# Regrouping the small steps around the first batch in the first stage of a two-layer kernel on one core

## The chip, the cores and the metric

The kernel runs on one core of a Trainium2 chip. The metric is the device time of one execution in microseconds (us). The core has five engines that run side by side, each with its own queue in program order: PE (TensorE, matrix products and transposes), DVE (VectorE), ACT (ScalarE), POOL (GpSimd) and SP, which here only issues DMAs. They wait for each other through semaphores.

## The reference

Two layers work on x of 4 batches x 1024 tokens x 128 columns. Each has an attention half and a feed-forward half, with modulation from a small product of c:

```python
mod = (silu(c) @ wmod)                       # six rows: sa, ca, ga, sb, cb, gb
h = layernorm(x) * (1 + ca) + sa
x = x + ga * attention(h)
h = layernorm(x) * (1 + cb) + sb
x = x + gb * ffn(h)
```

What the change touches is layer 0. Its attention is linear: Q = h W_Q^T, K = h W_K^T, M = K^T h, J = Q M / sqrt(128) + h, then a layernorm of J with gamma and beta. Its feed-forward is a choice of 2 of 8 experts for each token: gates = h gate_w^T + gate_b, the two largest, a softmax over the two, and for each chosen expert gelu(h w1 + b1) w2 + b2, weighted. Layer 1 (softmax attention over anchors, a gated ternary feed-forward) follows.

## The kernel before

**Stages.** From 0 to about 150 us the kernel does the first attention, the second norm and the routing of all four batches, and splits the expert weights into two parts. Then 23 tiles of rows, sorted by expert, go through the experts (to about 290 us). The rest is layer 1. All data of a batch is a tile of 128 partitions x 8 x 128 columns (`xa[:, b]`); a batch is handled in 8 column tiles, and most steps are in two halves g = 0, 1 of four tiles.

**Batch b of layer 0**, in the order of its dependences (engine in brackets):
- `first_stats(b)` [DVE]: 8 bn_stats of x, 8 bn_aggr, one addition of epsilon (`ve_L0a`). `rstd("L0a", b)` [POOL, L593]: the power -0.5. `minus_mean` [DVE, L1108]: `nmr_L0a`. `z_made(b)` [ACT, L737]: normalized rows z, 8 instructions; of batch 0 the first half is done by DVE (`half_normalized`, L1090).
- `z_transposed` [PE, L1653], `h0T_out` [ACT], `h0_back` [PE], `h0_out` [ACT], `gram` [PE, L1686], `gram_out` [ACT], `product` [PE, L1691], which gives P in PSUM. `first_half(b)` is ACT's part of this.
- `centred(b)` [DVE, L1116 to L1123]: `pm` and `pcat` from P. `jn_raw(b)` and `jn_centred(b)` [PE, L1703]. `beta(b)` [DVE, L1099] adds a row to `xa[:, b]`; for batch 1 POOL does it (L630) after the rows have come back from HBM.
- `inner_stats(b)` [DVE] on jn in PSUM, a root (`rstd("L0i", b)` on POOL for batches 0 and 1, Newton steps on DVE for 2 and 3), `residual_1(b)` [DVE, L1143], `second_stats(b)` [DVE], a root (POOL for batch 0, DVE for the others), `minus_mean` (`nmr_L0b`), `zb_made(b)` [ACT], `zb_transposed` [PE], `h1T_out` [ACT], `gates(b)` [PE, L1735].
- `choose(b)` [DVE, L1155 to L1170]: 14 small instructions to the chosen experts (`sel`). `ranks(b)` [PE]. `positions(b)` [DVE, L1186 to L1192]: `pos`. `scatter(b, ts)` [POOL, L601]: 16 indirect DMAs that write the rows of h1 to `rows_by_expert` in HBM.

**Expert weights.** They come in four quarters: SP loads `raw[q % 2]`, ACT rounds it (`expert_hi(q)`, 128 x 2048), DVE subtracts (`remainders(q, i)`, L1279, two operations of 128 x 1024), SP stores the parts to `w_split`. SP loads quarter q + 2 only behind the store of quarter q.

**Order.** Every queue's order is written out by hand. On DVE the steps of batch 0 are interleaved with statistics of later batches, the tables for routing, and `remainders(0, 0)` and `(0, 1)`; from batch 1 on there is a loop. On POOL the roots of all batches stand ahead of scatter(0), and nothing but the 64 scatters follows until layer 0's expert stage. SP issues all loads one after another: silu's input, `wm` in two halves, `xa[0]`, eight small ones (`gateb` is the last, and PE's `ww` product, L1769, waits for all of them), `xa[1..3]`, then `raw`.

## Time and profile before

| | us |
|---|---|
| median of 3 runs | 786.03 (785.18 to 786.83) |
| the profiled execution | 785.84 |
| its span, first to last instruction | 784.1 |

| engine | busy us | share of the span | instructions |
|---|---|---|---|
| PE | 656.5 | 84% | 2985 |
| DVE | 570.3 | 73% | 1443 |
| ACT | 400.9 | 51% | 698 |
| POOL | 271.5 | 35% | 227 |

The page's second part cuts the span into 40 slices of 19.6 us. In the first seven PE is busy 5, 5, 7, 7, 8, 4 and 1 tenths, and its granted clock falls from 9 to 5 and 6 tenths in the slices from 78 to 137 us; from about 150 us on PE is the busiest engine nearly throughout. So a share of 84% says little of the first stage, and it has to be read from timelines and from the chain of waits. Times count from the span's start.

### The profile page before, as it was taken

Reading aid. Unit: us, or ns where it says so; the run is one execution under the profiler, and the core shown is the slowest. Engines: PE = TensorE matmul, PEld = TensorE weight load, DVE = VectorE, ACT = ScalarE, POOL = GpSimd, SP = SyncE. Lnnn points to the kernel's source line nnn. Section 1 sums busy time; section 2 is a strip of 40 time slices with the busy share of each in tenths; the row PEclk is TensorE's granted clock in tenths of the full one; section 3 lists DMA queues with packets and bytes.
Section 4 is the critical chain, followed back from the end, with each engine's and each line's share of the span. In section 5 each row is a group of like instructions: output and inputs, shape, how many; then the busy total and the mean of one; then the engine's idle time right before and its main releaser. Section 6 shows DMA issues by size and latency. Waiting matters only on the chain.

```text
span 784.1 us, 9644 instructions
## 1 busy us (share of the span) xinstructions
PE 656.5 (84%) x2985; PEld 474.0 (60%) x2985; DVE 570.3 (73%) x1443; ACT 400.9 (51%) x698; POOL 271.5 (35%) x227
## 2 busy tenths in 40 slices
PE   5577841199999995679989899999899899899897
PEld 3467731178888874345468656468555478556575
DVE  4988767568877746976977686976786866793763
ACT  3455443167777742325276444375444485452573
POOL 6346767400000016687202276202475220341100
PEclk9896655589999995889999999999999999999999
DMA  5631277778899721000000000000100000000000
GB/s 210 206 101 45 108 277 288 252 254 266 268 280 337 229 80 31 23 21 20 8 1 0 34 21 28 1 0 1 37 24 22 0 1 1 27 1 1 0 1 28
DMA packets 25780, 69.26 MB, mean 88 GB/s; under 512 B 5297, under 2 KB 8385, under 8 KB 24385
## 3 DMA queue, kind: packets, MB, share of 16 engines
q1 hardware_dynamic: 21632, 60.24, 22.3%
q0 software_dynamic: 4096, 8.40, 3.4%
q8 instruction: 25, 0.41, 0.2%
q14 instruction: 27, 0.21, 0.1%
HBM read 46.46 MB, written 22.16 MB: 88 GB/s over the span
## 4 chain that ended last, share of the span: by engine, by line
PE 61%; DVE 21%; issue 5%; ACT 4%; POOL 4%; DMA 3%; SPq 1%; DVEq 0%; ACTq 0%; POOLq 0%
PE ps L1657 15%; PE ps L1653 9%; PE ps L1659 8%; PE ps L1661 6%; PE ps L1660 6%; PE ps L1913 6%; DVE stats L1051 3%; POOL rows_by_expert L601 2%; PE ps L1901 2%; PE ps L1931 2%; DVE lsum L1506 2%; PE ps L1703 2%; DVE ring L1538 2%; DMA raw<-in_w 1%; DVE yb L1438 1%
## 5 line engine op out<-in xcount | busy, mean ns | idle before, releaser
L642 POOL DMA_INDIRECT yb<-y_by_expert,ypos x64 | 63.8, 997 | 158.3 <-DMA y_by_expert<-ysb 142.6
L1657 PE MATMUL ps<-hid,fh 128*128 128x512 f32 x256 | 103.3, 404 | 5.1 <-DVE hid L1522 5.1
L1659 PE MATMUL ps<-hid,fh 128*128 128x512 f32 x256 | 101.4, 396 | 0.0
L690 POOL TENSOR_TENSOR misc<-misc,ring 128x1024 f32<-128x1024 f32 x28 | 66.0, 2356 | 35.5 <-DVE ring L1512 30.4
L601 POOL DMA_INDIRECT rows_by_expert<-h,pos x64 | 68.9, 1076 | 25.3 <-issue 18.5
L1522 DVE TENSOR_TENSOR hid<-ring,hid 128x512 fp32r<-128x512 f32 x56 | 38.6, 689 | 41.3 <-ACT hid L930 39.7
L1657 PEld LDWEIGHTS ps<-hid,fh 128*128 128x128 f32 x256 | 48.1, 188 | 20.9 <-DVE hid L1522 10.4
L1913 PE MATMUL ps<-ring,hn 128*128 128x512 f32 x112 | 55.4, 617 | 5.0 <-DVE ring L1512 5.0
L1931 PE MATMUL ps<-attnT,cmat 128*128 128x512 f32 x128 | 56.9, 593 | 0.0
L987 ACT ACTIVATE ring<-ps 128x1024 f32<-128x1024 f32 x32 | 32.8, 1024 | 44.2 <-PE ps L1901 44.0
L1659 PEld LDWEIGHTS ps<-hid,fh 128*128 128x128 f32 x256 | 48.2, 188 | 10.5
L1491 DVE TENSOR_REDUCE nmax<-ps 128x16 f32<-128x1024 f32 x32 | 39.1, 1221 | 18.1 <-PE ps L1661 18.1
L716 ACT ACTIVATE attnT<-ps 128x512 f32<-128x512 f32 x64 | 36.9, 597 | 21.0 <-PE ps L1653 20.2
L1403 DVE TENSOR_TENSOR hid<-ring,hid 128x512 fp32r<-128x512 f32 (+1 forms) x46 | 28.1, 610 | 26.5 <-ACT hid L725 26.5
L1060 DVE TENSOR_TENSOR hid<-ring,hid 128x512 fp32r<-128x512 f32 (+1 forms) x70 | 44.7, 639 | 2.4
L1506 DVE TENSOR_REDUCE lsum<-ring 128x16 f32<-128x1024 f32 x32 | 38.9, 1214 | 5.7 <-ACT ring L987 5.4
L929 ACT ACTIVATE ring<-ps,fs 128x512 f32<-128x512 f32 x32 | 22.0, 686 | 40.4 <-PE ps L1659 40.0
L1653 PE MATMUL ps<-ident,ring 128*128 128x128 f32 x224 | 33.1, 278 | 7.5 <-DVE hTa L1477 7.3
L1931 PEld LDWEIGHTS ps<-attnT,cmat 128*128 128x128 f32 x128 | 23.7, 191 | 25.0 <-issue 23.9
L1512 DVE TENSOR_TENSOR ring<-ring,lrec 128x1024 f32<-128x1024 f32 x28 | 37.8, 1350 | 1.0
L1657 PE MATMUL ps<-hT,wbuf 128*128 128x512 f32 (+1 forms) x92 | 34.8, 378 | 3.3 <-issue 1.6
L1653 PEld LDWEIGHTS ps<-ident,ring 128*128 128x128 f32 x224 | 25.5, 142 | 18.9 <-issue 18.8
(323 smaller groups left out, 1681.2 us busy)
## 6 DMA issues: line engine op xcount, KB each, us to landing
wbuf<-w_split SPq DMA_DIRECT2D x46, 512.0 KB, 5.4
w_split<-parts SPq DMA_DIRECT2D x4, 2048.0 KB, 7.0
raw<-in_w SPq DMA_DIRECT2D x8, 512.0 KB, 8.9
xs<-rows_by_expert SPq DMA_DIRECT2D x16, 256.0 KB, 5.6
y_by_expert<-ysb SPq DMA_DIRECT2D x16, 256.0 KB, 4.8
ffn_raw<-in_ffn SPq DMA_DIRECT2D x1, 2816.0 KB, 11.2
rows_by_expert<-zeros SPq DMA_DIRECT2D x9, 256.0 KB, 2.3
xa<-in_x SPq DMA_DIRECT2D x4, 512.0 KB, 6.3
```

The costliest lines, as they stand in the source:

```text
L601: gp.indirect_dma_start(disp, bass.IndirectOffsetOnAxis(pos[:, b, k, t:t + 1].bitcast(U32), 0), h1[:, b % 2, t, :], None).then_inc(scatter ...
L642: gp.indirect_dma_start(yb[:, k, t, :], None, ydisp, bass.IndirectOffsetOnAxis(ypos[:, b, k, t:t + 1].bitcast(U32), 0))\
L690: gp.tensor_tensor(asum, asum, ring[:, 2 * (t % 2):2 * (t % 2) + 2, :] .rearrange("p a n -> p (a n)"), ALU.add).then_inc(*pool_asum.raise_(t))
L1060: v.tensor_tensor(dst_lo, src, f(dst_hi), ALU.subtract).then_inc(*ev.raise_(job))
L1506: settle(b, v.tensor_reduce(lsum[:, :], exponentials(t), X, ALU.add))
L1653: last_ = te.transpose(ps[0:rows_, bank, i * 128:(i + 1) * 128], s, ident[:, :])
L1657: te.matmul(out_, w(0), x(0), start=first, stop=False)
L1659: return te.matmul(out_, w(0), x(1), start=False, stop=last_)
L1660: te.matmul(out_, w(0), x(1), start=False, stop=False)
L1661: return te.matmul(out_, w(1), x(0), start=False, stop=last_)
L1913: last_ = te.matmul(ps[:, 6 + h, :], hn[:, t, :], attention(t, h), start=t == 0, stop=t == T - 1)
L1931: last_ = te.matmul(ps[:, 2 + g, :], cmat[:, k, :], attnT[:, k, g * GW:(g + 1) * GW], start=k == 0, stop=k == AC - 1)
```

## The change

It reorders layer 0's work around batch 0 and 1:

- SP: `xa[0]` is loaded ahead of the first `wm`, `xa[1]` ahead of the second `wm` and the small loads.
- DVE: `first_stats` is cut in two, `first_stats` (bn_stats) and `first_sums` (bn_aggr and epsilon), with a second buffer `next_stats`. The bn_stats of batch 1 stand ahead of batch 0's `norm_ready`, those of batch 2 behind `first_sums(1)`; `first_sums(2)` stands between `inner_stats(0)` and `residual_1(0)`; `first_stats(3)` and `first_sums(3)` move ahead of `choose(0)`. `residual_1(0)`, `second_stats(0)` and `centred(1)` move ahead of the `modt` columns. Tables that routing needs later (`thr`, `unit`, `upto`) move behind batch 1's `norm_ready`, `onehot` behind `y_positions`. `residual_1(1)` is in two halves around `positions(0)`.
- POOL: it takes over both remainders of quarter 0 (behind `zb` of batch 0), and the roots of `L0a` for batch 2 and of `L0b` for batch 0 change places around the addition to `xa[1]`.
- ACT: `z_made(2)` stands behind `first_half(1)`, `z_made(3)` behind `h1_out` of batch 0, each one batch sooner.
- PE: `jn_raw(1)` goes ahead of `zb_transposed(0)`, `jn_centred(1)` is in two halves, `gates` waits for each half of h1T by itself, and `z_transposed(2, 0)` goes behind `ranks(0)`.

```diff
@@ SP
             load(silu[:, :], ins["cT"], l_mod)
+            load(xa[:, 0], by_tile(ins["x"][0]), l_x[0])
             load(wm[:, 0, :], ins["wmod"][:, 0:768], l_mod)
-            load(xa[:, 0], by_tile(ins["x"][0]), l_x[0])
+            load(xa[:, 1], by_tile(ins["x"][1]), l_x[1])
             load(wm[:, 1, :], ins["wmod"][:, 768:1536], l_mod1)
...
             for q in range(4):
-                sp.wait_ge(*w_lo.done((q, 1)))
+                sp.wait_ge(*(w_lo if q else pool_lo).done((q, 1)))
@@ POOL
             rstd("L0i", 0)
-            rstd("L0b", 0)
+            rstd("L0a", 2)
             pool.wait_ge(l_rows, 16)
             pool.wait_ge(*act_z.done((1, 1)))
             gp.tensor_tensor(xa[:, 1], xa[:, 1], over_tiles(R_GBETA, 1, T), ALU.add).then_inc(pool_beta, 1)
-            rstd("L0a", 2)
+            rstd("L0b", 0)
+
+            pool.wait_ge(*zb_done(0, 0))
+            pool.wait_ge(*w_hi.done(0))
+            for i in range(2):
+                gp.tensor_tensor(parts[0][:, :, i, 1, :], raw[0][:, i], f(parts[0][:, :, i, 0, :]), ALU.subtract)\
+                    .then_inc(*pool_lo.raise_((0, i)))
             rstd("L0i", 1)
             rstd("L0a", 3)
@@ ACT
             first_half(1)
+            z_made(2)
...
-                if b + 2 < B:
-                    z_made(b + 2)
+                if b == 0:
+                    z_made(3)
                 tanh(b)
@@ DVE
+            def first_sums(b, of=stats):
+                if b:
+                    dve.wait_ge(*dve_nmr["L0a"].done(b - 1))
+                if b == 1:
+                    dve.wait_ge(*z_done(0, 0))
+                aggregated("rows", "L0a", 0, T, of).then_inc(*dve_var["L0a"].raise_(b))
...
             first_stats(0)
+            first_sums(0)
...
+            first_stats(1)
             norm_ready("L0a", 0)
             half_normalized("L0a", z, "z")
...
-            first_stats(1)
+            first_sums(1)
+            first_stats(2, next_stats)
...
             inner_stats(0)
-            remainders(0, 0)
+            first_sums(2, next_stats)
+            residual_1(0)
+            minus_mean("L0a", 2)
+            second_stats(0)
+            centred(1)
...
-            residual_1(0)
-            second_stats(0)
+            norm_ready("L0b", 0)
+            half_normalized("L0b", zb, "zb")
...
-            remainders(0, 1)
-            norm_ready("L0b", 0)
-            half_normalized("L0b", zb, "zb")
-            centred(1)
-            v.tensor_copy(onehot[:, :], oh_f[:, :])
-            first_stats(2)
-            inner_stats(1)
...
-            norm_ready("L0a", 2)
             choose(0)
-            first_stats(3)
+            minus_mean("L0a", 3)
+            residual_1(1, (0,))
             positions(0)
-            residual_1(1)
-            norm_ready("L0a", 3)
+            residual_1(1, (1,))
             second_stats(1)
             norm_ready("L0b", 1)
...
             y_positions()
+            v.tensor_copy(onehot[:, :], oh_f[:, :])
@@ PE
             product(1)
+            jn_raw(1)
             for g in gs2:
                 zb_transposed(0, g)
-            jn_raw(1)
+            jn_centred(1, (0,))
             pe.wait_ge(*dve_setup.done("jv"))
             gates(0)
-            jn_centred(1)
```

(`inner_stats(1)`, `first_stats(3)` and `first_sums(3)` follow the tables `order`, `erow` and `tot`, ahead of `choose(0)`.)

## Rows read from the trace of the kernel before

**Rows 1.** Chain that ended last, in order of time: start us, us, what.
```profile
95.08 10.43 DMA raw<-in_w
...
146.73 2.82 DMA rows_by_expert<-h,pos
```
**Rows 2.** Timeline of POOL: start us, us, engine line op out<-in xcount [idle before <-releaser].
```profile
53.75 1.24 POOL L601 DMA_INDIRECT rows_by_expert<-h,pos  x1 [0.21 <-issue]
...
76.82 0.96 POOL L601 DMA_INDIRECT rows_by_expert<-h,pos  x1 [1.99 <-DVE pos L1192]
...
101.51 0.96 POOL L601 DMA_INDIRECT rows_by_expert<-h,pos  x1 [3.87 <-DVE pos L1192]
...
123.80 0.95 POOL L601 DMA_INDIRECT rows_by_expert<-h,pos  x1 [0.92 <-DVE pos L1192]
```
**Rows 3.** Timelines of DVE and ACT, first loads; columns as above.
```profile
7.69 1.64 DVE L1051 BATCH_NORM_STATS2 stats<-xa 128x6 f32<-128x128 f32 x8 [7.69 <-DMA xa<-in_x]
...
12.00 0.37 DVE L1108 SCALAR_TENSOR_TENSOR nmr_L0a<-mv_L0a,rs_L0a 128x8 f32<-128x8 f32 x1 [1.64 <-POOL rs_L0a L593]
...
6.33 0.21 ACT L798 ACTIVATE silu<-silu 128x8 f32<-128x8 f32 x1 [4.26 <-DMA wm<-in_wmod]
```
**Rows 4.** Timeline of PE.
```profile
13.62 0.49 PE L1769 MATMUL ps<-wkq 128*128 128x128 f32 x2 [1.23 <-DMA gateb<-in_gate_b]
```
**Rows 5.** Timelines of POOL and DVE, 10 to 38 us.
```profile
10.31 1.66 POOL L593 TENSOR_TENSOR rs_L0a<-ve_L0a,neghalf 128x8 f32<-128x8 f32 x1 [4.45 <-DVE ve_L0a L1056]
...
25.46 2.55 POOL L593 TENSOR_TENSOR rs_L0i<-ve_L0i,neghalf 128x8 f32<-128x8 f32 x1 [5.98 <-DVE ve_L0i L1056]
...
34.52 2.71 POOL L630 TENSOR_TENSOR xa<-xa,rows 128x1024 f32<-128x1024 f32 x1
...
25.29 1.22 DVE L1279 TENSOR_TENSOR parts<-raw,parts 128x1024 fp32r<-128x1024 f32 x1
...
28.11 2.16 DVE L1143 SCALAR_TENSOR_TENSOR xa<-ps,rs_L0i,xa 128x128 f32<-128x128 f32 x8 [1.05 <-issue]
...
32.67 0.17 DVE L1056 TENSOR_SCALAR ve_L0b<-mv_L0b 128x8 f32<-128x8 f32 x1
...
34.95 2.30 DVE L1108 SCALAR_TENSOR_TENSOR nmr_L0b<-mv_L0b,rs_L0b 128x8 f32<-128x8 f32 x1
```
**Rows 6.** The instructions of line 1495: durations ns min/median/max, first and last start.
```profile
L1495 DVE CAST m<-nmax x32: 174/304/2991, 311.3 to 700.8; 128x16 fp32r<-128x16 f32 x32
```
**Rows 7.** Timeline of DVE, 45 to 60 us.
```profile
45.88 0.22 DVE L1155 TENSOR_TENSOR gt<-ps,gateb 128x64 f32<-128x64 f32 x1
...
49.29 1.65 DVE L1051 BATCH_NORM_STATS2 stats<-xa 128x6 f32<-128x128 f32 x8
...
52.63 0.17 DVE L1192 CAST pos<-posf 128x16 int32<-128x16 f32 x1
...
59.72 0.17 DVE L1108 SCALAR_TENSOR_TENSOR nmr_L0b<-mv_L0b,rs_L0b 128x8 f32<-128x8 f32 x1
```
**Rows 8.** Timeline of PE; then windows: busy of each engine, granted clock, DMA, GB/s.
```profile
60.66 3.79 PE L1703 MATMUL ps<-pm,h0T 128*128 128x128 f32 x16 [4.12 <-DVE pm L1116]
...
84.89 2.05 PE L1703 MATMUL ps<-pm,h0T 128*128 128x128 f32 x16 [0.38 <-DVE pm L1116]
...
50.00:60.00 10.00, 5.95 (x43) 4.81 (x43) 9.33 (x59) 6.27 (x12) 6.67 (x6) 0.98 0.09 29
60.00:66.00 6.00, 5.34 (x24) 5.09 (x24) 3.91 (x17) 3.77 (x9) 4.77 (x5) 0.50 0.13 44
```
**Rows 9.** Timelines of DVE and ACT, 64 to 85 us.
```profile
64.58 1.68 DVE L1051 BATCH_NORM_STATS2 stats<-ps 128x6 f32<-128x128 f32 x8 [1.95 <-PE ps L1703]
...
84.54 0.29 DVE L1116 SCALAR_TENSOR_TENSOR pm<-ps,ident 128x128 f32<-128x128 f32 x1 [3.00 <-PE ps L1691]
...
73.91 3.17 ACT L737 ACTIVATE z<-xa,nmr_L0a,rs_L0a 128x128 f32<-128x128 f32 x8
```
**Rows 10.** Timeline of DVE, start of the expert stage.
```profile
153.29 0.42 DVE L1393 TENSOR_TENSOR hT<-ps,hT 128x256 fp32r<-128x256 f32 x1 [7.10 <-ACT hT L725]
```

More of the change, by code:

```diff
@@ L297, in build @@
         pool_beta = sem("pool_beta")
-        w_hi, w_lo = Once(sem("w_hi"), range(4)), Once(sem("w_lo"), [(q, i) for q in range(4) for i in range(2)])
+        w_hi, w_lo = Once(sem("w_hi"), range(4)), Once(sem("w_lo"), [(q, i) for q in range(1, 4) for i in range(2)])
+        pool_lo = Once(sem("pool_lo"), [(0, i) for i in range(2)])
         f_hi, f_lo = Once(sem("f_hi"), range(4)), sem("f_lo")
@@ L469, in _ @@
                 load(dst, src, l_small)
-            for b in range(1, B):
+            for b in range(2, B):
                 load(xa[:, b], by_tile(ins["x"][b]), l_x[b])
@@ L1099, in beta, with first_stats @@
                 settle("rows", v.tensor_tensor(xa[:, b], xa[:, b], row, ALU.add))
-            def first_stats(b):
+            def first_stats(b, to=stats):
                 dve.wait_ge(l_x[b], 16)
-                norm_stats("rows", "L0a", 0, [xa[:, b, t, :] for t in ts]).then_inc(*dve_var["L0a"].raise_(b))
+                tile_stats("rows", [xa[:, b, t, :] for t in ts], to)
+            def first_sums(b, of=stats):
[4 more added lines that the diff above has]
+                aggregated("rows", "L0a", 0, T, of).then_inc(*dve_var["L0a"].raise_(b))
             def minus_mean(k, b):
@@ L1133, in inner_stats, with residual_1 @@
                 norm_stats("rows", "L0i", 0, [jn(t, 2) for t in ts]).then_inc(*dve_var["L0i"].raise_(b))
-            def residual_1(b):
-                if b == 1:
+            def residual_1(b, halves=gs2):
+                if b == 1 and 0 in halves:
                     dve.wait_ge(pool_beta, 1)
-                if b < POOL_ROOTS["L0i"]:
+                if b < POOL_ROOTS["L0i"] and 0 in halves:
                     dve.wait_ge(*pool_rs["L0i"].done(b))
-                for g in gs2:
+                for g in halves:
                     dve.wait_ge(*pe_jn.done((b, g)))
@@ L1145, in residual_1 @@
                     last.then_inc(*dve_x1.raise_((b, g)))
-                dve.wait_ge(*dve_x1.done((b, 1)))
+                if 1 in halves:
+                    dve.wait_ge(*dve_x1.done((b, 1)))
             def second_stats(b):
@@ L1328, in _ @@
             settle("setup", v.tensor_copy(jv[:, :], ps[:, 6, 128:160]))
-            residual_1(0)
-            second_stats(0)
+            norm_ready("L0b", 0)
+            half_normalized("L0b", zb, "zb")
             v.tensor_scalar(order[:, :], jv[:, 0:E], -1.0, float(E), ALU.mult, ALU.add)
             v.tensor_scalar(erow[:, :], jv[:, 0:E], float(REGION), None, ALU.mult)
-            v.tensor_scalar(thr[:, :], jv[:, 0:E], float(GW), None, ALU.mult)
-            v.tensor_scalar(tot[:, :], jv[:, 0:E], 0.0, None, ALU.mult)
-            settle("setup", v.tensor_scalar(unit[:, :], jv[:, 0:NT], 0.5, WIDE / 2.0, ALU.mult, ALU.add))
-            v.tensor_tensor(unit[:, :], unit[:, :], jv[:, 0:NT], ALU.min)
-            v.tensor_tensor(upto[:, :, :], jv[:, 0:2 * E].unsqueeze(1).broadcast_to([128, 2 * E, 2 * E]),
-                            jv[:, 0:2 * E].unsqueeze(2).broadcast_to([128, 2 * E, 2 * E]), ALU.is_le)\
-                .then_inc(*dve_setup.raise_("jv"))
-            dve.wait_ge(*dve_setup.done("jv"))
-            remainders(0, 1)
-            norm_ready("L0b", 0)
-            half_normalized("L0b", zb, "zb")
-            centred(1)
-            v.tensor_copy(onehot[:, :], oh_f[:, :])
-            first_stats(2)
-            inner_stats(1)
+            v.tensor_scalar(tot[:, :], jv[:, 0:E], 0.0, None, ALU.mult).then_inc(*dve_setup.raise_("jv"))
+            inner_stats(1)
+            first_stats(3)
+            first_sums(3)
+            dve.wait_ge(*dve_setup.done("jv"))
             def both(q):
@@ L1351, in both @@
                     remainders(q, i)
-            norm_ready("L0a", 2)
             choose(0)
-            first_stats(3)
+            minus_mean("L0a", 3)
+            residual_1(1, (0,))
             positions(0)
-            residual_1(1)
-            norm_ready("L0a", 3)
+            residual_1(1, (1,))
             second_stats(1)
             norm_ready("L0b", 1)
+            v.tensor_scalar(thr[:, :], jv[:, 0:E], float(GW), None, ALU.mult)
+            settle("setup", v.tensor_scalar(unit[:, :], jv[:, 0:NT], 0.5, WIDE / 2.0, ALU.mult, ALU.add))
+            v.tensor_tensor(unit[:, :], unit[:, :], jv[:, 0:NT], ALU.min)
+            settle("setup", v.tensor_tensor(upto[:, :, :], jv[:, 0:2 * E].unsqueeze(1).broadcast_to([128, 2 * E, 2 * E]),
+                                            jv[:, 0:2 * E].unsqueeze(2).broadcast_to([128, 2 * E, 2 * E]), ALU.is_le))
             for b in range(1, B):
@@ L1712, in jn_raw, with jn_centred @@
                     rows_times(b, 2, pm[:, b % 2, :], g, pe_raw)
-            def jn_centred(b):
+            def jn_centred(b, halves=gs2):
                 pe.wait_ge(*dve_pcat.done(b))
-                for g in gs2:
+                for g in halves:
                     if b:
```

19 lines of the change are left out of this document (12 added, 7 removed).

## The prediction

> **What bounds the kernel now.** The span is 784.1 us, and behind 152 us PE is the chain; the change touches only what lies ahead of the first expert tile. So the views to read are those of 0 to 160 us. First the chain in order of time: DVE steps, then the `raw` load of the fourth quarter of expert weights, then POOL's scatters; the last lands 2.82 us after 146.73, and only then can the first expert tile come [rows 1]. So two streams set the end: the dependent steps over DVE, ACT and PE that give `pos` of each batch, and POOL's 64 scatters, which need `pos`. Second, POOL's timeline: batches of scatters start at 53.75, 76.82, 101.51 and 123.80, with 1.99, 3.87 and 0.92 us idle before the last three [rows 2]. About 0.3 us of each is the ordinary spacing, so POOL has 5.9 us to give; what goes beyond must come from an earlier scatter(0). Third, DVE's timeline, where each idle time names what is late.
>
> **The loads.** `xa[0]` now comes ahead of the first `wm`, and `xa[1]` ahead of the second and of all small loads. DVE idles 1.64 us before batch 0's `nmr_L0a` [rows 3]; the bn_stats of batch 1 now fall there, those of batch 2 take their old place, and DVE's work up to `pm` of batch 0 stays the same. But PE's `ww` product waits for the last small load, `gateb`, at 13.62 [rows 4], and all of batch 0 is behind it. One more issue and 512 KB now go ahead of `gateb`. Bounds: +0.4 us if only the issue counts, and +1.4 us if the bytes count (`xa[0]`, as large, landed 1.36 us behind `wm` [rows 3]). I take **+0.6**: `gateb` came alone, long after its neighbours' bytes, so it is nearer to the first.
>
> **Batch 0 up to nmr_L0b.** Before, `remainders(0,0)` (1.22 us at 25.29) ran while POOL wanted `rs_L0i`: POOL took 2.55 us where its root before took some 1.65 (10.31 to 11.97), and DVE idled 1.05 before `residual_1(0)` at 28.11 [rows 5]. The remainder is gone, and `first_sums(2)` fits beside the root: **-0.95**. New on POOL, ahead of `rstd("L0b",0)`, is `rstd("L0a",2)`, about 1.65, and with it the `xa[1]` addition comes sooner: 2.71 us at 34.52 before [rows 5], of which some 2.2 are its own (DVE's remainder held it back until 35.0). It will run from about 29.4 to 31.6, and DVE wants `minus_mean("L0a",2)` at 29.9. The trace shows what such a meeting costs: `nmr_L0b`, on 8 columns, took 2.30 us from 34.95, just until POOL's addition ended [rows 5]. So **+1.9** (bounds 0, if DVE is first, and 2.2). `ve` of `second_stats(0)` then ends at 34.3 instead of 32.84. Before, 4.4 us passed from there to the end of `nmr_L0b` at 37.25, with the second remainder and POOL's addition in the way [rows 5]. Now it waits for the root alone, 1.65, beside which `centred(1)` and the `modt` columns fit: 1.9, **-2.55**. Sum 0.6 - 0.95 + 1.9 - 2.55 = -1.0: `nmr_L0b(0)` at 36.2.
>
> A rule of the Trainium skill speaks against this regrouping: "SBUF — State Buffer", section "Who interferes with whom", calls the ports that VectorE shares with GpSimd an exclusive lock, which copies, casts and tensor_scalar within SBUF need as well as operations with two SBUF inputs. The trace agrees for two inputs (2.30 us) and for a cast, median 304 ns and at most 2991 [rows 6]; for the `ve` tensor_scalar no row shows it.
>
> **From zb to choose(0).** `remainders(0,*)` go to POOL behind `zb`: two operations of 2.2 to 2.7 us by the addition's row, 37.4 to about 42. Queued behind them on POOL are the roots `L0i`(1) and `L0a`(3) and scatter(0); `L0a`(3) would end near 46.5, before DVE asks. SP's queue waits for them with the store of quarter 0 and the `raw` loads of quarter 2 behind it, some 7 us later than now; ACT wants these only at 75. PE does `jn_raw(1)` ahead of `zb`'s transposes, which therefore come some 0.3 to 1 us behind `zb`. DVE has `order`, `erow`, `tot`, `inner_stats(1)`, `first_stats(3)` and `first_sums(3)`, 5.2 us, and waits some 0.9 for `jn_raw(1)` by these times. One of these DVE steps may be caught by POOL: bounds 0 and 2.2 us, I take 1.1, halfway, since nothing shows which of the two comes first. `choose(0)` starts at 44.3 instead of 45.88 [rows 7]. With no catch it would be 43.5, where PE's `gates(0)` are due too.
>
> **choose(0) to nmr_L0b(1).** `first_stats(3)`, 2.44 us from 49.29 on with its bn_aggr, is out of this stretch; `thr`, `unit`, `upto` (0.75) move behind it; `positions(0)` waits 0.3 for PE's ranks and lies between the halves of `residual_1(1)`. So `pos(0)` comes at 50.2 instead of 52.8 [rows 7], scatter(0) starts at 51.0 instead of 53.75 [rows 2], and `nmr_L0b(1)` ends at 56.3 instead of 59.9 [rows 7]: **-3.6**. With the tables, `centred(2)` comes at 57.5, and `jn_raw(2)` on PE at 57.9 instead of 60.66 [rows 8]: -2.8.
>
> **ACT.** `z_made(3)` takes the slot of `z_made(2)` ahead of `first_half(2)`, 3.2 us each, so P of batch 2 comes near 56.5, as before: just not late. `expert_hi(1)` ends at 57.9, then comes `zb_made(1)`, 2 us sooner than now; `gates(1)` then end near 64, and DVE needs them at 64.6.
>
> **jn_raw(2).** It took 3.79 us at 60.66, with a granted clock of 0.50 from 60 to 66 us, the lower level, 1.2 GHz; the same work took 2.05 at 84.89, and 50 to 60 us had 0.98 [rows 8]. PE had stood idle 4.1 us ahead of it. Now the gap is 1.4 us, and I expect the higher level: `inner_stats(2)` at 60.0 instead of 64.58 [rows 9], **-4.6**; at the lower one, -2.8.
>
> **Batch 3's first half.** DVE waited 3.00 us for P(3) until 84.54, because ACT made `z(3)` only from 73.91 on (3.17 us) and another 7.4 us went by to P [rows 9]. Now z(3) is there 20 us sooner, and its transposes start behind `ranks(1)`, near 69.5. With the old 7.4 us, at half clock in part, and 1.1 for the first transposes, P(3) comes at 78; without it near 75.5. DVE asks at 77.0. Wait left 0 to 1.0; I take 0.5: **-2.5**.
>
> **The rest.** From there the order is the old one and each trigger moves along; `raw`'s last load (10.43 us [rows 1]) is asked for behind `remainders(1,1)`. The fourth batch of scatters gains 4.6 + 2.5 = 7.1 and starts at 116.7. POOL on its own, from 51.0, needs 70.05 us to that point less its 5.9 idle, 115.2 [rows 2]: not the bound, by 1.5 us. `onehot`'s cast (0.67) now lies ahead of the weight splits; DVE idles 7.10 us before its first expert tile [rows 10], which covers it, and it would cost 0.6 without. The stages behind move along unchanged. **Sum 7.1 us.** The profiled execution took 785.84; the median of three, 786.03, is 0.2 above: 785.84 - 7.1 + 0.2 = **778.9**.
>
> **Rivals.** (a) *Most of batch 0's gain is lost and the clock stays low*: `gateb` +1.4, DVE caught in full, `jn_raw(2)` at 3.79 us. Then 3.6 - 0.8 - 1.1 = 1.7 at `nmr_L0b(1)`, 0.9 at `centred(2)`, and with 0 for the clock and 3.0 for the early z(3) 3.9: 782.1. For it: the 2.30 us row; against: DVE's gaps there are mostly PSUM steps. (b) *Nothing catches DVE*, `gates(0)` are the bound at 43.5, P(3) is in time: 7.1 + 0.8 + 0.5 = 8.4, 777.6; POOL's own bound is then 9.4. (c) *The gain is hidden*, because the expert stage waits for another thing, such as the `w_split` stores and the weights of its first tile: 786.0. Against: the chain goes over the scatters [rows 1]. (d) *Slower, by POOL's remainders*. No row shows this form (two inputs in pieces, fp32r out). Roots `L0i`(1) and `L0a`(3) are queued behind them, and behind `L0a`(3) DVE stands at `minus_mean("L0a",3)` with `positions(0)` and batch 1. DVE asks at 47.8, so 7.1 us of lateness, which undoes the whole gain, are reached where the two end at 51.6: from 7.1 us an operation on, instead of 2.3. At 9 us each they end at 55.4 and `L0a`(3) at 58.7, 10.9 late: 789.8. Against: the addition of this size at 2.2 to 2.7. "GPSIMD Engine Reference", section 3.1, of the skill gives 4.5 us for 2048 elements, so 2.2 for 1024 as an estimate; by it too (d) is unlikely.
>
> **Chances.** Forecast (778.0 to 780.4) 0.50; (a) 0.25; (b) 0.12; (c) 0.07; (d) 0.06. The range, 776.3 to 784.0, holds the first three with their bounds and leaves 0.13 out. A measurement of this kernel can tell 0.2%, 1.6 us, from no change: faster 0.87, same 0.07, slower 0.06.
>
> **What would show it.** `ww` at 14.0 to 14.4; `minus_mean("L0a",2)` stretched to 1.5 us or more; POOL's two `parts` at 2.2 to 2.7 us; `choose(0)` at 43.5 to 45.5; the first scatter at 51; no half-clock `jn_raw(2)`; no 3 us of idle before `pm` of batch 3; the fourth batch of scatters at 116.7; first expert transposes near 145, and behind them the same 632 us as now. The prediction is wrong if POOL's root of `L0a`(3) ends later than `choose(0)`, or if a DVE step of batch 1 waits for ACT.

## The result and the profile after

| | before | after |
|---|---|---|
| median, us | 786.03 (783.06 to 787.64, 7 runs) | 781.12 (779.58 to 786.98, 7 runs) |
| after / before | | 0.9943, 95% interval 0.9921 to 0.9965 |
| on another chip | 787.34 (784.3 to 791.44, 12 runs) | 779.94 (778.87 to 781.55, 6 runs), ratio 0.9914, 0.989 to 0.994 |
| the profiled execution, its span | 785.84, 784.1 | 786.98, 785.2 |
| busy PE, DVE, ACT, POOL | 656.5, 570.3, 400.9, 271.5 | 658.9, 569.2, 400.8, 276.2 |

The forecast was 778.9 in 776.3 to 784.0; measured is 781.12: by the medians 4.9 us less where 7.1 were forecast, by the ratio 0.57%. The profiled execution of after is the slowest of its seven, 5.9 us above their median. So its span says nothing against before's 784.1. The excess lies behind the first stage: from DVE's first split of an expert tile, defined below, to the end of the span, after's execution needs 636.2 us, before's 630.8, and the second execution of after 630.6. The times up to that split can therefore be laid beside before's.

POOL's timeline, the first scatter of each batch (start us, us, engine line op out<-in xcount, idle before):

```profile
51.48 1.24 POOL L605 DMA_INDIRECT rows_by_expert<-h,pos  x1 [5.82 <-DVE pos L1216]
...
72.46 0.95 POOL L605 DMA_INDIRECT rows_by_expert<-h,pos  x1 [0.31 <-issue]
...
95.41 0.96 POOL L605 DMA_INDIRECT rows_by_expert<-h,pos  x1 [2.67 <-DVE pos L1216]
...
117.09 0.96 POOL L605 DMA_INDIRECT rows_by_expert<-h,pos  x1 [0.30 <-issue]
```

Against [rows 2] they come 2.27, 4.36, 6.10 and 6.71 us sooner, and before the second and the fourth POOL now only keeps its ordinary 0.30 us: there POOL is the bound. It binds by little: from DVE's `pos` to the first scatter 1.17 and 1.12 us go by, where before had 0.95 both times. Up to here 6.7 of the 7.1 forecast us have arrived. The next fence is the end of the same timeline, then DVE's beside it, then SP's load of the first expert rows and PE's first transposes:

```profile
134.32 5.83 POOL L605 DMA_INDIRECT rows_by_expert<-h,pos  x1 [0.31 <-issue]
...
133.04 0.73 DVE L1408 CAST onehot<-oh_f 32x1024 fp32r<-32x1024 f32 x1
133.70 1.21 DVE L1414 TENSOR_TENSOR fab<-ffn_raw,fab 128x1024 fp32r<-128x1024 f32 x1
134.83 4.47 DVE L1414 TENSOR_TENSOR fh<-ffn_raw,fh 128x2048 fp32r<-128x2048 f32 x2
139.24 0.67 DVE L1414 TENSOR_TENSOR fy<-ffn_raw,fy 128x512 fp32r<-128x512 f32 x1
148.99 0.42 DVE L1420 TENSOR_TENSOR hT<-ps,hT 128x256 fp32r<-128x256 f32 x1 [9.08 <-ACT hT L735]
...
145.75 0.33 SPq L458 DMA_DIRECT2D xs<-rows_by_expert  x1
...
147.77 0.69 PE L1680 MATMUL ps<-ident,xs 128*128 128x128 f32 x2 [30.82 <-DMA xs<-rows_by_expert]
```

One scatter takes 5.83 us instead of 0.96. It begins while DVE does the first of the four subtractions that split the weights, and ends at 140.15, behind the last of them (139.91). In before the same subtractions lay there too, and two scatters took 3.02 and 1.89:

```profile
139.92 1.27 DVE L1387 TENSOR_TENSOR fab<-ffn_raw,fab 128x1024 fp32r<-128x1024 f32 x1
141.12 4.48 DVE L1387 TENSOR_TENSOR fh<-ffn_raw,fh 128x2048 fp32r<-128x2048 f32 x2
...
141.20 3.02 POOL L601 DMA_INDIRECT rows_by_expert<-h,pos  x1 [0.31 <-issue]
144.53 1.89 POOL L601 DMA_INDIRECT rows_by_expert<-h,pos  x1 [0.30 <-issue]
```

From the first to the end of the last of the last 16 scatters, after needs 26.85 us (117.09 to 143.94) and before 23.89 (123.80 to 147.69): 3.0 us of the gain go there. DVE's first split of an expert tile (`hT` into two parts, the first DVE step of the expert stage) comes at 148.99 instead of 153.29 [rows 10], 4.3 us sooner.

The steps of batch 0, on DVE and POOL:

```profile
27.36 2.16 DVE L1166 SCALAR_TENSOR_TENSOR xa<-ps,rs_L0i,xa 128x128 f32<-128x128 f32 x8 [1.01 <-POOL rs_L0i L597]
29.55 1.70 DVE L1131 SCALAR_TENSOR_TENSOR nmr_L0a<-mv_L0a,rs_L0a 128x8 f32<-128x8 f32 x1
...
35.53 0.17 DVE L1131 SCALAR_TENSOR_TENSOR nmr_L0b<-mv_L0b,rs_L0b 128x8 f32<-128x8 f32 x1 [0.23 <-POOL rs_L0b L597]
...
40.24 1.27 DVE L1068 TENSOR_SCALAR ve_L0i<-mv_L0i 128x8 f32<-128x8 f32 x1
...
43.85 0.23 DVE L1179 TENSOR_TENSOR gt<-ps,gateb 128x64 f32<-128x64 f32 x1
...
28.89 2.34 POOL L634 TENSOR_TENSOR xa<-xa,rows 128x1024 f32<-128x1024 f32 x1
...
36.81 4.68 POOL L640 TENSOR_TENSOR parts<-raw,parts 128x1024 fp32r<-128x1024 f32 x2 [1.38 <-DVE zb L1106]
```

Two operations on 8 columns are stretched, `nmr_L0a` of batch 2 to 1.70 us beside POOL's addition and `ve_L0i` of batch 1 to 1.27 beside POOL's `parts`; by themselves such operations take 0.17.

### The profile page after: what moved, and what is told of

It is laid out like the page before. It is cut to its first block, busy times and chain, and to the rows that moved or that the text cites. A ratio compares the mean times of both kernels' runs of the same rounds, so it can differ in the third digit from the quotient of the medians.

```text
span 785.2 us, 9648 instructions
## 1 busy us (share of the span) xinstructions
PE 658.9 (84%) x2985; PEld 476.0 (61%) x2985; DVE 569.2 (72%) x1441; ACT 400.8 (51%) x698; POOL 276.2 (35%) x229
## 4 chain that ended last, share of the span: by engine, by line
PE 60%; DVE 23%; POOL 6%; issue 5%; ACT 3%; DMA 1%; SPq 0%; DVEq 0%; ACTq 0%; POOLq 0%
PE ps L1684 15%; PE ps L1680 8%; PE ps L1686 8%; PE ps L1688 6%; PE ps L1687 6%; PE ps L1941 6%; POOL rows_by_expert L605 5%; DVE stats L1061 3%; PE ps L1929 2%; PE ps L1959 2%; DVE lsum L1533 2%; DVE ring L1565 2%; PE ps L1730 1%; DVE yb L1465 1%; DVE cmat L1640 1%
## 5 line engine op out<-in xcount | busy, mean ns | idle before, releaser
L605 POOL DMA_INDIRECT rows_by_expert<-h,pos x64 | 70.9, 1107 | 27.4 <-issue 18.9
L1680 PE MATMUL ps<-ident,xs 128*128 128x128 f32 x78 | 13.0, 284 | 30.8 <-DMA xs<-rows_by_expert 30.8
```

What stands on the lines that cost most here:

```text
L605: gp.indirect_dma_start(disp, bass.IndirectOffsetOnAxis(pos[:, b, k, t:t + 1].bitcast(U32), 0), h1[:, b % 2, t, :], None).then_inc(scatter ...
L1680: last_ = te.transpose(ps[0:rows_, bank, i * 128:(i + 1) * 128], s, ident[:, :])
```

## The experiments

Each was timed in rounds with the kernel before on the same chip. They are told in the order in which they ran, four on one chip at a time: the first four on one, the next four on a second, the last four on a third. What the traces showed in the end, one execution each, us from the span's start ("split" is DVE's first `hT` of the experts, batch 3 the fourth batch):

| kernel | 1st scatter, batch 0 | 1st scatter, batch 3 | last scatter ends | longest of the last 16 | split | median | ratio to before, interval |
|---|---|---|---|---|---|---|---|
| before | 53.75 | 123.80 | 147.69 | 3.02 | 153.29 | | |
| after | 51.48 | 117.09 | 143.94 | 5.83 | 148.99 | 781.12 | 0.9943, 0.9921 to 0.9965 |
| after, again | 50.96 | 115.15 | 141.43 | 5.83 | 146.55 | 779.94 | 0.9914, 0.989 to 0.994 |
| gate by a semaphore | 51.45 | 116.86 | 142.49 | 5.83 | 147.54 | 780.98 | 0.9925, 0.9897 to 0.9952 |
| addition later | 50.33 | 114.31 | 140.86 | 5.83 | 145.91 | 778.14 | 0.9896, 0.9864 to 0.9928 |
| cast earlier | 52.78 | 117.19 | 141.29 | 3.03 | 146.35 | 780.00 | 0.991, 0.9884 to 0.9936 |
| z(3) at its old place | 51.02 | 115.29 | 141.90 | 5.83 | 146.98 | 781.36 | 0.9927, 0.9896 to 0.9958 |
| before, new loads | 56.34 | 126.75 | 150.64 | 3.03 | 157.18 | 788.08 | 1.0011, 0.999 to 1.0033 |
| after, gated | 50.97 | 116.89 | 138.34 | 1.98 | 146.50 | 779.33 | 0.9899, 0.9861 to 0.9937 |
| before, gated | 55.42 | 123.77 | 144.64 | 1.41 | 151.83 | 782.66 | 0.9929, 0.9901 to 0.9958 |

The intervals are 3.4 to 6.0 us wide, so effects of 1 to 3 us are read from the stages and not from the medians. One kernel's executions differ by some 2 us there too, as the two rows of after show.

**The changed kernel again.**

> The changed kernel once more, as the base of the other runs. Seen so far: in its trace the fourth batch of scatters starts at 117.09 us (before: 123.80, 6.7 sooner) but the first expert transposes at 147.77 (before 152.07, 4.3 sooner), because the sixteen last scatters took 3.0 us more; one of them took 5.83 us while DVE did the four subtractions that split the layer 1 weights (133.7 to 139.9). Theory A (DVE's two-input operations shut POOL out of descriptor writing, and where they fall decides how much): the long scatters come again at the splits, in sum 3 to 6 us over 16 x 1.26. Theory B (a chance of one execution): the last 16 scatters take 22.9 us as before and the first transposes come near 145. Time by A: 4 to 5 us under the kernel before; by B about 7.

The ratio is 0.9914 and the long scatter comes back with the same length:

```profile
131.80 5.83 POOL L605 DMA_INDIRECT rows_by_expert<-h,pos  x1 [0.31 <-issue]
```

So it is no accident of one execution. The time, 6.8 us less by the ratio, is nevertheless nearer to the 7 of theory B, because the scatters started sooner than in the first execution, the fourth batch at 115.15 instead of 117.09. Ahead of none of the three later batches does POOL wait here (0.30 us each time): from its first scatter on POOL alone sets the pace. The same holds for the executions with the addition later and with the cast earlier.

What changed from the first execution to this one is P(3)'s product `jn_raw(3)` on PE, the first line below in after, the second here. It is the same work behind nearly the same gap, once mostly at the lower clock level and once at the higher; the granted clock from 76 to 81 us was 0.66 and 1.00:

```profile
76.96 3.65 PE L1730 MATMUL ps<-pm,h0T 128*128 128x128 f32 x16 [1.89 <-DVE pm L1139]
```

```profile
76.92 2.05 PE L1730 MATMUL ps<-pm,h0T 128*128 128x128 f32 x16 [1.92 <-DVE pm L1139]
```

**Subtractions behind the scatters, first try: a semaphore raised from POOL's queue.**

```diff
             for b in bs:
                 scatter(b, ts)
+            pool.sem_inc(all_issued, 1)
...
+            dve.wait_ge(all_issued, 1)
             for i in range(4):
```

> DVE starts the four weight splits only when POOL has issued the last scatter. Theory A (lock): no scatter of the last batch over 2.1 us, those after 133 us all at 0.96; the last scatter starts near 138 instead of 142.98, and the first expert transposes near 143 to 144.5 instead of 147.8 (the splits, 6.2 us, then end near 145 and ACT's first hT waits for them, so some of the gain may stay there): 2.5 to 4 us faster than the changed kernel. Rival B (the long scatter is the DMA queue, which carries 2 MB of zeros and the first expert weights from 128 to 141 us): scatters between 134 and 141 us stay long, and the time gets worse by the 1 to 2 us that the splits end later.

The experiment failed: the gate held nothing. DVE's first subtraction still began at 133.53, with scatters on POOL until 142.49, and the one at 134.14 took 5.83 us. The increment behind the last scatter in the queue was done before POOL had worked the scatters off. It decides nothing between the theories.

**POOL's addition to the rows of batch 1 behind zb of batch 0.**

```diff
             rstd("L0a", 2)
-            pool.wait_ge(l_rows, 16)
-            pool.wait_ge(*act_z.done((1, 1)))
-            gp.tensor_tensor(xa[:, 1], ...).then_inc(pool_beta, 1)
             rstd("L0b", 0)
             pool.wait_ge(*zb_done(0, 0))
+            pool.wait_ge(l_rows, 16)
+            pool.wait_ge(*act_z.done((1, 1)))
+            gp.tensor_tensor(xa[:, 1], ...).then_inc(pool_beta, 1)
             pool.wait_ge(*w_hi.done(0))
```

> POOL's addition to xa[1] goes behind zb of batch 0, ahead of its two remainders. By the lock theory nmr_L0a(2), 1.70 us long in the changed kernel (29.55 to 31.2), falls to 0.2 and everything on DVE to choose(0) comes 1.5 us sooner; the three POOL operations then run from 35.3 to 42.4 and may catch one DVE instruction (ve_L0i, 1.27 us now). pos(0) 1 to 1.5 us sooner. At the end of the stage 0.5 to 1.5 us, if DVE's order is the bound there; rival (POOL's stream is the bound from batch 1 on, its idle time before the third batch is 2.67): the early scatters only wait longer between batches 1 and 2, and the fourth batch starts within 0.5 us of 117.1. Time: 0 to 1.5 us under the changed kernel.

```profile
29.91 0.17 DVE L1131 SCALAR_TENSOR_TENSOR nmr_L0a<-mv_L0a,rs_L0a 128x8 f32<-128x8 f32 x1
...
34.34 0.17 DVE L1131 SCALAR_TENSOR_TENSOR nmr_L0b<-mv_L0b,rs_L0b 128x8 f32<-128x8 f32 x1 [0.22 <-POOL rs_L0b L597]
...
38.20 2.12 DVE L1068 TENSOR_SCALAR ve_L0i<-mv_L0i 128x8 f32<-128x8 f32 x1
...
42.71 0.21 DVE L1179 TENSOR_TENSOR gt<-ps,gateb 128x64 f32<-128x64 f32 x1
```

`nmr_L0a` of batch 2 is no longer caught, `nmr_L0b` of batch 0 comes 1.19 us sooner than in after, and `choose(0)` 1.14 sooner although `ve_L0i` is now stretched to 2.12. Against the changed kernel on the same chip the two come 1.6 and 1.5 us sooner. The catch that the prediction priced at 1.9 us is real; the place of the addition was worth about 1 us, and all four batches of scatters keep it (0.6 to 1.1 us against the changed kernel on the same chip). The median is the lowest of all, but its interval overlaps the changed kernel's.

**The one-hot cast ahead of choose(3).**

```diff
+                if b == B - 1:
+                    v.tensor_copy(onehot[:, :], oh_f[:, :])
                 choose(b)
...
             y_positions()
-            v.tensor_copy(onehot[:, :], oh_f[:, :])
```

> onehot's cast (0.73 us just ahead of the weight splits) goes ahead of choose of batch 3, where DVE idles 4.9 us. It is hidden there, so the splits come 0.7 us sooner against the scatters. Theory A1 (the place of the splits against the scatter grid decides, and the one cast moved by the change is what made it worse): the last 16 scatters fall back from 25.9 to about 23 us, 2 to 3 us faster. Theory A2 (any place gives about the same, between 3 and 5 us lost over the splits): within 1 us of the changed kernel.

```profile
132.26 1.27 DVE L1415 TENSOR_TENSOR fab<-ffn_raw,fab 128x1024 fp32r<-128x1024 f32 x1
133.45 4.48 DVE L1415 TENSOR_TENSOR fh<-ffn_raw,fh 128x2048 fp32r<-128x2048 f32 x2
...
133.53 3.03 POOL L605 DMA_INDIRECT rows_by_expert<-h,pos  x1 [0.31 <-issue]
136.87 1.90 POOL L605 DMA_INDIRECT rows_by_expert<-h,pos  x1 [0.30 <-issue]
```

With the cast out of the tail, the lengths of before are there again, 3.03 and 1.90. The last 16 scatters take 24.10 us instead of 26.28 (the changed kernel, again), and the split follows the batch's start by 29.16 us instead of 31.40: 2.2 us won in the tail (the stretch from the fourth batch's first scatter to the split). This execution had begun late (`ww` at 15.20 us, first scatter at 52.78), so its split is only 0.2 us sooner, and the medians agree.

What separates 3.0 from 5.8 is where a scatter stands when the 2048-wide subtractions begin. In before, here and in before with the new loads it started 0.08 us, 0.08 and 0.09 behind them; in the five executions of the changed order that had the long one it started 0.51 to 0.52 ahead of them, under the 1024-wide one. The first kind got through after one of the large subtractions, the second waited for all. Why POOL gets in between two subtractions in one case and not in the other no run shows. Nor does a row of subtractions always do this: in after DVE also subtracts four times 128x1024 without a pause (99.84 to 104.46), and the two scatters beside them take 1.42 and 1.97 us.

```profile
99.84 4.62 DVE L1303 TENSOR_TENSOR parts<-raw,parts 128x1024 fp32r<-128x1024 f32 x4
...
102.20 1.97 POOL L605 DMA_INDIRECT rows_by_expert<-h,pos  x1 [0.30 <-issue]
```

**z(3) at its old place.**

```diff
-                if b == 0:
+                if b == 1:
                     z_made(3)
```

> The changed kernel with one edit undone: ScalarE makes z(3) in its old place, behind second tile work of batch 1 instead of batch 0. The prediction gave P(3)'s wait (3.0 us in the kernel before) to this move. Theory (the early z(3) earns its place): VectorE waits 2 to 3 us for TensorE ahead of the means of batch 3 (no wait in the changed kernel), the fourth batch of scatters starts 1.0 to 3.0 us later than in the changed kernel, and the time is 1.0 to 3.0 us above it: ratio to the kernel before 0.994 to 0.998. Rival (the wait is only moved: the chain of the fourth batch is set by the last load of raw weights and ScalarE's work behind it): the wait comes back, but the fourth batch of scatters starts within 0.5 us of the changed kernel's, and so does the time.

DVE's rows about P(3) here:

```profile
76.72 0.28 DVE L1139 SCALAR_TENSOR_TENSOR pm<-ps,ident 128x128 f32<-128x128 f32 x1
...
79.24 1.68 DVE L1061 BATCH_NORM_STATS2 stats<-ps 128x6 f32<-128x128 f32 x8 [0.21 <-PE ps L1730]
```

No wait comes back, and batch 3 starts at 115.29, as in the changed kernel on the first chip (115.15): neither the theory nor its rival had the wait right. ACT made z(3) from 67.33 instead of 73.91 [rows 9], since `zb_made(1)` and all behind it had come sooner; from there to P(3)'s own product 8.5 us went by as against 10.1 in before, because `gram(3)` on PE took 2.02 us where it had taken 3.62. So P(3) comes 8.2 us sooner than in before, while DVE asks for it 4.8 us sooner: the 3.0 us wait went with the earlier batch 1 and the higher clock, and needs no early z(3). That move is worth 1.2 us on PE (the product at 74.59 in after, 75.82 here) and nothing on the path: DVE's last `pos` comes 0.5 us later than in the changed kernel on the first chip (113.95 against 113.41), but POOL is still busy with the batch before it. Where the early z(3) does show is the gap ahead of `jn_raw(3)`: 1.6 to 1.9 us with it on the first two chips, 0.75 here without it, in one execution.

**The kernel before with the new order of the loads.**

```diff
             load(silu[:, :], ins["cT"], l_mod)
+            load(xa[:, 0], by_tile(ins["x"][0]), l_x[0])
             load(wm[:, 0, :], ins["wmod"][:, 0:768], l_mod)
-            load(xa[:, 0], by_tile(ins["x"][0]), l_x[0])
+            load(xa[:, 1], by_tile(ins["x"][1]), l_x[1])
             load(wm[:, 1, :], ins["wmod"][:, 768:1536], l_mod1)
```

> The kernel before with the new order of the first loads alone: the rows of batch 0 ahead of the first block of the modulation weights, the rows of batch 1 ahead of the second. Theory: gate_b's row lands within 1 us of where it did and the first real bound stays the pair of silu and the products, so that the time is within -0.3 to +0.8 us of the kernel before, and the scatters start within 0.5 us of theirs. Rival: the loads alone give a part of the 4.5 us (the statistics of batch 0 start 0.8 us sooner), then -0.8 us or more.

The interval, 0.999 to 1.0033, holds no gain over 0.8 us: the loads alone bring nothing. The scatters start 2.6 us later than in before, not within the 0.5 expected, but 1.7 of this also shows in the gated kernel before (55.42), which differs only in its last scatters: that much one kernel's executions differ. The loads cost at another place than I had thought. The first fence is PE here, the second in after:

```profile
9.28 5.28 PE L1766 MATMUL ps<-wm,silu 128*4 128x384 f32 x8
14.49 0.49 PE L1770 MATMUL ps<-wkq 128*128 128x128 f32 x2
```

```profile
9.26 4.23 PE L1793 MATMUL ps<-wm,silu 128*4 128x384 f32 x8
13.41 0.49 PE L1797 MATMUL ps<-wkq 128*128 128x128 f32 x2
```

Before, the products began at 7.54 and `ww` waited another 1.23 us for `gateb` [rows 4]. Now the modulation weights land behind the rows and the products begin 1.7 us later. `gateb` is no longer waited for; `ww` comes directly behind the products, at 13.3 to 15.2 in all executions with this order.

**The subtractions behind the scatters, by an operation of POOL.**

```diff
             for b in bs:
                 scatter(b, ts)
+            gp.memset(pace[:, :], 0.0).then_inc(all_issued, 1)
...
+            dve.wait_ge(all_issued, 1)
             for i in range(4):
```

> The changed kernel, and VectorE starts the four subtractions that split the weights of the first layer of layer 1 only when GpSimd has done a one-column memset that stands behind the last scatter in its queue. Theory (the subtractions lock GpSimd's descriptor work out; that is where 3 of the forecast 7.1 us went): the 5.8 us scatter is gone, none of the last 16 is over 2.2 us, their last one ends 22 us behind the start of their first (26.9 in the changed kernel); the subtractions then run 6.2 us alone, and VectorE's first split of the experts starts 28.5 to 29.5 us behind the first scatter of the batch (31.9 in the changed kernel): 2.4 to 3.4 us sooner, ratio to the kernel before 0.987 to 0.990. Rival (the long scatter has a cause of its own, a full ring or its data): it stays 5.8 us long though VectorE is idle beside it, the subtractions come behind it, and the time is 3 to 5 us above the changed kernel's.

POOL, DVE, SP and PE with the gate:

```profile
134.86 0.96 POOL L607 DMA_INDIRECT rows_by_expert<-h,pos  x1 [0.31 <-issue]
136.12 0.96 POOL L607 DMA_INDIRECT rows_by_expert<-h,pos  x1 [0.30 <-issue]
137.39 0.95 POOL L607 DMA_INDIRECT rows_by_expert<-h,pos  x1 [0.30 <-issue]
138.34 0.12 POOL L648 MEMSET pace<- 128x1 f32 x1
...
138.49 1.23 DVE L1418 TENSOR_TENSOR fab<-ffn_raw,fab 128x1024 fp32r<-128x1024 f32 x1 [5.44 <-POOL pace L648]
139.63 4.49 DVE L1418 TENSOR_TENSOR fh<-ffn_raw,fh 128x2048 fp32r<-128x2048 f32 x2
144.03 0.68 DVE L1418 TENSOR_TENSOR fy<-ffn_raw,fy 128x512 fp32r<-128x512 f32 x1
146.50 0.42 DVE L1424 TENSOR_TENSOR hT<-ps,hT 128x256 fp32r<-128x256 f32 x1 [1.78 <-ACT hT L738]
...
143.21 0.33 SPq L460 DMA_DIRECT2D xs<-rows_by_expert  x1
...
145.27 0.69 PE L1684 MATMUL ps<-ident,xs 128*128 128x128 f32 x2 [29.16 <-DMA xs<-rows_by_expert]
```

With DVE idle beside the last scatters they take 0.96 us, the longest of the batch (1.98, earlier) is within the 2.2 expected, the last 16 take 21.45 us, and the cause of the long scatter is shown: the subtractions. Of the 5.4 us that POOL gets back against after (26.85) the split keeps only 2.3 (29.61 us behind the batch's start instead of 31.90; 1.8 against the 31.40 of the second execution of after), less than the 2.4 to 3.4 expected. SP asked for the first expert rows 4.9 us behind the last scatter's end, where it had been 1.8 in after: the scatters leave sooner and land later. SP stood waiting for the scatters' landing there (5.1 us). That the DMA engines are the next bound fits: from 12 us behind the batch's start on they carry the eight zero fills of 256 KB and the first expert weights, and behind the last scatter they were 0.95 busy from 138 to 140 us, 0.69 to 142 and 0.01 to 144, where after had 0.21 in the two us in which its last scatter ended. No run takes this traffic away, so it stays argued. In time the ratio is 0.9899, against 0.9914 for the changed kernel on the first chip: not distinguishable.

**The same gate in the kernel before.**

> The kernel before with the same gate: its four subtractions start behind GpSimd's memset that follows the last scatter. Theory: the two long scatters of 3.02 and 1.89 us become 0.96, the last one ends 21 us behind the first (23.9 in the kernel before), the subtractions end 27.3 behind it and the time falls by 1.0 to 2.4 us, less than what the same gate gives in the changed kernel; with both gated, the changed kernel is 6 to 7.5 us below this one, which is what the prediction had for the scatters' starts. Rival (the tail is not where the gain was lost): the gate gives the same in both and the two gated kernels differ by the 4.5 to 6.8 us by which the two kernels differ without it.

The last scatter ends 20.87 us behind the first (23.89 before), the split follows by 28.06 instead of 29.49: 1.4 us, in the expected range and less than the 2.3 of the changed kernel. Between the two gated kernels the batch starts differ by 6.88 us and the splits by 5.33; ungated, by 6.71 and 4.30. So the subtractions account for about 0.9 of the 2.4 us that the tail swallowed, and 1.55 stay without them; against the second execution of after it is 0.4 of 1.9. Of the 1.55, 0.6 are in the scatters themselves (21.45 against 20.87) and 0.9 between the last one's end and SP's load (4.87 against 3.96). The 6 to 7.5 us expected between the gated kernels are there at the starts and not at the splits, so the theory names one of at least two causes. The median fell by 4.2 us against the 1.0 to 2.4 expected, more than the trace can place, and the two gated kernels' medians differ by 3.3 us, less than either theory had; both remain open.

**The kernel before with the cast in the tail.**

```diff
             y_positions()
+            v.tensor_copy(onehot[:, :], oh_f[:, :])
...
             centred(1)
-            v.tensor_copy(onehot[:, :], oh_f[:, :])
```

> The kernel before with one piece of the change: the one-hot cast goes behind the result positions, directly ahead of the four subtractions. Theory (what counts is where the subtractions meet the grid of the scatters): VectorE's 1024-wide subtraction starts 16.8 us behind the first scatter of the batch (16.1 in the kernel before) and the 2048-wide ones 18.0 us behind it; a scatter starts at 17.4, so it is under way when they begin, and lasts 5.8 us as in the changed kernel instead of 3.0 and 1.9 for two; the last scatter ends 25.8 to 26.9 us behind the first (23.9) and the first split of the experts comes 31 to 32 us behind it (29.5). The time is +0.5 to +2.5 us against the kernel before (0.7 us less work of VectorE in batch 0, 2 us more at the end). Rival (the long scatter belongs to the changed kernel's stages, not to the place of the cast): the scatters stay at 3.0 and 1.9 us, the time is -0.7 to 0 us.

This and the next three ran on the third chip, where the kernel before took 810.03 us (803.29 to 815.75). Its traces have stretches between 60 and 150 us where PE, DVE and ACT stand at once and no releaser is shown, once with POOL too (100.7 to 103.4 here); DVE's subtractions began at 164.31, 4.3 us behind the last scatter's end (159.99), so that they could lock nothing. The ratio of 1.0002 (0.9974 to 1.0031) says nothing on the grid: inconclusive. The first 55 us are undisturbed on this chip, and from the next three I read only these and the tail of one.

**The modulation weights ahead of the rows again.**

```diff
-            load(xa[:, 0], by_tile(ins["x"][0]), l_x[0])
             load(wm[:, 0, :], ins["wmod"][:, 0:768], l_mod)
+            load(xa[:, 0], by_tile(ins["x"][0]), l_x[0])
```

> The changed kernel with the first block of the modulation weights ahead of the rows of batch 0 again, the rows of batch 1 still ahead of the second block. Theory (putting the rows first costs the chain of the weights): ScalarE's silu and the products start at 6.3 to 6.9 us instead of 8.1 to 9.0, the keys' product ww at 12.9 to 13.7 instead of 13.4 to 15.2, each batch of scatters starts 0.5 to 1.2 us sooner than in the other executions of the changed kernel (50.96 to 52.8 for the first), ratio to the kernel before 0.989 to 0.993. Rival (the statistics of batch 0 become the bound in their place, or gate_b's row does): ww stays at 13.4 or later and nothing moves.

`ww` comes at 12.91, as expected, but the first scatter at 51.07, hardly sooner than the 50.96 to 51.48 of most executions of the changed kernel: the theory's 0.5 to 1.2 us are missed. With the rows later, `nmr_L0a` of batch 0 is at 12.07 instead of 11.19 (11.2 to 12.0 in all kernels with the rows first), so one gain, of at most 0.9 us, is traded for another. The rival named this, though `ww` did move. The ratio is 0.9911 (0.987 to 0.9952), like the changed kernel's. The tail of this trace shows the long scatter once more, started 0.64 us ahead of the large subtractions:

```profile
149.83 4.47 DVE L1414 TENSOR_TENSOR fh<-ffn_raw,fh 128x2048 fp32r<-128x2048 f32 x2
...
149.19 5.96 POOL L605 DMA_INDIRECT rows_by_expert<-h,pos  x1 [0.30 <-issue]
```

**Addition later and gate together, and these two with the weights first.**

> The changed kernel with both edits that earned something: GpSimd's addition to the rows of batch 1 goes behind VectorE's norm of batch 0's second statistics, and the four subtractions wait for GpSimd's memset behind the last scatter. Theory (the two gains lie in different stages and add up): scatters start at 50.3, 71.3, 92.7 and 114.4 us, none over 2.2 us long, first split of the experts at 143.7 to 144.5 us; the time is 3 to 4.5 us below the changed kernel's, ratio to the kernel before 0.985 to 0.989. Rival (the DMA engines bind the tail now): scatters start as said, but the first split of the experts comes at 145 us or later, ratio 0.989 to 0.991.

> The same two edits and the weights' first block ahead of the rows. Theory: 0.5 to 1.2 us below the kernel with the two edits, from the loads; scatters start at 49.3 to 49.8 us; ratio to the kernel before 0.984 to 0.988. Rival: the loads are worth nothing once the other two are in, and the two kernels agree within 0.5 us.

Ratios 0.9936 (0.9904 to 0.9968) and 0.993 (0.9899 to 0.9961), no better than the changed kernel's on the first chip and short of the 0.984 to 0.989 expected. The first scatter starts at 49.71 and 49.48 us, against 51.07 for the kernel with the weights first alone on the same chip: the later addition gives 1.6 us up to there (0.6 on the first chip), and the order of the loads 0.2. The standing times behind, such as this one on PE in the kernel with two edits, are as large as what is looked for, and whether the two gains add up stays open:

```profile
65.00 1.85 PE L1767 MATMUL ps<-gatew,h1T 128*128 128x8 f32 x8 [4.43 <-issue]
```

## Why the prediction was right, and where it was not

- **What bounds the stage**: right. The chain of after goes over the same scatters, from 95 us on over nothing else, and the gain of each batch's first scatter is the gain of `pos` until POOL binds.
- **The loads, +0.6**: the sum came out near zero in after (`ww` 13.41 instead of 13.62), and the mechanism was wrong. It is not `gateb` that is later but the modulation weights; by all executions of the new order on the first two chips the term is between -0.4 and +1.6 us. The old order has `ww` at 13.62, 13.09 and 12.14 in its three executions, so after's near zero was chance and the term rather too small. The order also buys an earlier `nmr_L0a`.
- **Batch 0**: right. The root runs unheld (1.64 us, forecast 1.65), `nmr_L0a` of batch 2 is caught for 1.70 us (forecast 1.9), `nmr_L0b` comes at 35.53 (36.2), and one more catch is there at 1.27 us (forecast 1.1). `choose(0)` came at 43.85 (44.3). The rule of the Trainium skill, "SBUF — State Buffer", section "Who interferes with whom", that tensor_scalar can contend for the shared ports as well had no row in before. The traces agree: `ve_L0i` of batch 1 took 1.26 to 2.12 us instead of 0.17 in all ten executions with POOL's `parts` beside it.
- **choose(0) to nmr_L0b(1)**: right. The first scatter starts at 51.48 (51.0), `nmr_L0b` of batch 1 at 56.19 (56.3). POOL's root `L0a`(3) ended at 45.66, before `choose(0)` was through at 47.24, so this sign of a wrong prediction did not appear.
- **jn_raw(2) at the higher clock**: right, 2.05 us at 57.98 in after (57.9 forecast) and in all traces of the changed order on the first two chips but one (2.55), where it had been 3.79 [rows 8].
- **P(3), -2.5**: the size was near and the reason wrong. At `pm` of batch 3 after is 7.9 us ahead (76.63 against 84.54), 3.5 more than at `inner_stats(2)`; 1.6 of it are lost again right behind. DVE does not wait for P(3), but the run with z(3) in its old place does not either. And the next product, `jn_raw(3)`, fell to the lower level in after and in two further executions (3.2 to 3.65 us), and not in others, with gaps of 1.6 to 1.9 us ahead of it in both (0.75 with z(3) at its old place); of the seven executions of the changed order on the first two chips, the three that fell are those in which `jn_centred(2)`, some 13 us earlier, had taken 3.4 to 3.6 us and not 2.03. That cost after 1.79 us of waiting, which the prediction had not seen.
- **POOL is not the bound, by 1.5 us**: wrong. In after it binds at the second and the fourth batch by 0.2 us. In the second execution of after, where `jn_raw(3)` was at the higher level, it binds from its first scatter on, and the fourth batch starts at 115.15: this is the 115.2 that the prediction had worked out for POOL alone. From there on only an earlier first scatter or shorter scatters can gain.
- **The fourth batch at 116.7**: 117.09.
- **"The stages behind move along unchanged", and the cast covered by 7.10 us of idle**: the step that failed. The cast has the cover on DVE, but what counts is POOL beside it: the cast and the subtractions meet the scatters 0.4 us later in their spacing, a scatter of 5.83 us stands where 3.02 and 1.89 were, and the last 16 take 3.0 us more. The term for the tail was 0 and measured +2.4 us at the split (6.71 less 4.30). Taking the cast away gives 2.2 of it back, though with the subtractions gated in both kernels 1.55 remain; the two readings don't add up to one number, and come from one execution each. Behind the split the stages did move along unchanged, 629.9 to 632.2 us in all traced executions on the first two chips but after's own.
- **Rivals**: (a) is near in time (782.1) and not in its mechanism, as neither catch nor clock failed. (c) holds in part: what was lost, was lost behind the scatters' starts. (b) and (d) didn't come: `choose(0)` was not bound by `gates(0)`, and POOL's `parts` took 2.34 us each.

The median sum, 786.03 - 4.3, would be 781.7 by this execution's stages; 781.12 was measured. The other chip's 6.8 us go with an execution in which `jn_raw(3)` was at the higher level and the split came 6.74 us sooner than in before. That this is so near to the forecast 7.1 is luck: its fourth batch started 8.65 us sooner, and the tail took 1.9 of it, two errors that nearly cancel.

## What to carry to other kernels

An idle engine ahead of a wait is not free cover when another engine works beside it: ask of every filler whom it locks out, not only who waits for it, and read the lengths of the other engine's instructions in the stretch where it will lie. Where a chain of one engine's many small DMA issues sets the end, keep the wide two-input operations of DVE out of it, or put them behind it; here that gave 1.8 to 2.3 us at the split, too little to tell in the time. When two causes are credited for one wait that vanished, undo them singly; here the edit made for it was not the one that removed it.

## What the runs showed of the hardware

- An indirect DMA on POOL that takes 0.96 us alone took 1.1 to 2.1 us beside most wide DVE operations, rows of four 128x1024 subtractions among them. It took 5.83 to 5.96 where it had started 0.5 to 0.6 us ahead of two 128x2048 subtractions, fp32 in and fp32r out, and 3.02 or 3.03 where it had started just behind their beginning. The Trainium skill, "SBUF — State Buffer", section "Who interferes with whom", has tensor_tensor not stall DMA, and marks the reason as inferred. Here the measurement decides: with DVE gated the long scatters were gone in both kernels.
- A semaphore increment in POOL's queue behind the scatters acted before they were worked off; a one-column memset (0.12 us) at the same place started as the last scatter ended.
- The same product, behind gaps of 1.6 to 1.9 us, was granted either level in executions of the same order of work (2.05 us or 3.2 to 3.65).
